# Six straight-line copies of the batch body become one hardware loop, on each of five engines

## The reference

```
x = x + 0.5 * ffn(layernorm(x))       # w_gate, w_up: 2048 x 512, w_down: 512 x 2048
x = x + attn(layernorm(x))            # 16 heads of 32, causal, unit-norm q and k,
x = x + 0.5 * ffn(layernorm(x))       # rotary embedding on the even heads, a gain per head

ffn(x)  = (silu(x @ w_gate.T) * (x @ w_up.T)) @ w_down.T
attn(x) = softmax(causal(q @ k.T * gain)) @ v @ w_out
```

## Time and profile before

| | |
|---|---|
| median of 3 runs | 3007.3 us (3006.99 to 3007.64) |
| the profiled execution | 3007.3 us, of which 3005.5 us lie between its first and its last instruction (the span) |
| instructions recorded | 56592 |
| PE | 2820.8 us busy, 94%, 23744 matmuls |
| PEld | 2056.7 us busy, 68% |
| DVE | 1806.0 us busy, 60%, 4252 instructions |
| ACT | 1222.2 us busy, 41%, 2218 instructions |
| POOL | 407.0 us busy, 14%, 438 instructions |
| DMA | 37.31 MB moved, of them 3.06 MB and 0.55 MB on the two queues of the kind "instruction" |

### The profile page before, as it was taken

How to read it: one execution, slowest core, us unless ns; L and a number is a source line. 1 busy time by engine, 2 the same in 40 slices (tenths; PEclk the granted TensorE clock), 3 DMA queues, 4 the chain that set the end, 5 groups by cost and what they waited for, 6 DMA issues and landing times.

```text
span 3005.5 us, 56592 instructions
## 1 busy us (share of the span) xinstructions
PE 2820.8 (94%) x23744; PEld 2056.7 (68%) x23744; DVE 1806.0 (60%) x4252; ACT 1222.2 (41%) x2218; POOL 407.0 (14%) x438
## 2 busy tenths in 40 slices
PE   4799999999999999999999999999999999999999
PEld 3576766676767667676776667776677676776666
DVE  8656766775357753667447674476634766357743
ACT  5233553552236522454225542254423553235522
POOL 0103203110022000220002200112002020021000
PEclk8899999999999999999999999999999999999999
DMA  6000000000000000000000000000000000000000
GB/s 240 15 1 1 2 1 1 8 1 22 1 1 9 7 17 1 1 8 22 1 1 1 8 22 1 1 1 8 22 1 1 8 1 22 1 1 9 1 8 15
DMA packets 15486, 37.31 MB, mean 12 GB/s; under 512 B 1408, under 2 KB 1408, under 8 KB 14720
## 3 DMA queue, kind: packets, MB, share of 16 engines
q1 hardware_dynamic: 15232, 33.70, 3.2%
HBM read 25.31 MB, written 8.39 MB: 11 GB/s over the span
## 4 chain that ended last, share of the span: by engine, by line
PE 66%; DVE 16%; ACT 9%; issue 6%; POOL 3%; DMA 0%; ACTq 0%; SPq 0%; DVEq 0%
PE psum L860 20%; PE psum L861 19%; PE psum L862 19%; ACT arena L567 5%; DVE mneg L771 3%; DVE arena L792 3%; ACT arena L563 2%; PE psum L905 1%; DVE arena L727 1%; PE psum L1016 1%; PE psum L968 1%; DVE arena L716 1%; PE psum L972 1%; DVE arena L723 1%; POOL rn L450 1%
## 5 line engine op out<-in xcount | busy, mean ns | idle before, releaser
L860 PE MATMUL psum<-arena,WG 128*128 128x256 f16 x2048 | 561.0, 274 | 14.7 <-DVE arena L716 14.7
L862 PE MATMUL psum<-arena,WG 128*128 128x256 f16 x2048 | 561.8, 274 | 0.0
L861 PE MATMUL psum<-arena,WG 128*128 128x256 f16 x2048 | 561.5, 274 | 0.0
L860 PE MATMUL psum<-arena,WU 128*128 128x256 f16 x2048 | 560.8, 274 | 0.0
L861 PE MATMUL psum<-arena,WU 128*128 128x256 f16 x2048 | 560.3, 274 | 0.0
L862 PE MATMUL psum<-arena,WU 128*128 128x256 f16 x2048 | 560.2, 274 | 0.0
L721 DVE SCALAR_TENSOR_TENSOR arena<-arena,psum 128x256 f32<-128x256 f32 x512 | 214.1, 418 | 493.2 <-ACT arena L578 492.6
L578 ACT ACTIVATE arena<-psum,tscale 128x256 f32<-128x256 f32 x512 | 242.4, 473 | 621.2 <-PE psum L862 620.7
L860 PE MATMUL psum<-WD,arena 128*128 128x512 f16 x1024 | 389.5, 380 | 38.9 <-DVE arena L727 38.9
L862 PE MATMUL psum<-WD,arena 128*128 128x512 f16 x1024 | 388.6, 379 | 0.0
L861 PE MATMUL psum<-WD,arena 128*128 128x512 f16 x1024 | 388.6, 379 | 0.0
(11 more groups left out here) (143 smaller groups left out, 4674.0 us busy)
## 6 DMA issues: line engine op xcount, KB each, us to landing
arena<-in_L_attn_x SPq DMA_DIRECT2D x16, 512.0 KB, 3.8
out<-arena SPq DMA_DIRECT2D x16, 512.0 KB, 2.8
arena<-in_L_ffn_w_gate SPq DMA_DIRECT2D x4, 1024.0 KB, 9.0
arena<-in_L_ffn_w_up SPq DMA_DIRECT2D x4, 1024.0 KB, 8.3
WD<-in_L_ffn_w_down SPq DMA_DIRECT2D x4, 1024.0 KB, 10.6
arena<-in_L_attn_w_qkv SPq DMA_DIRECT2D x1, 3072.0 KB, 20.8
WQ<-in_L_attn_w_out SPq DMA_DIRECT2D x1, 1024.0 KB, 23.1
ropet<-rope_table SPq DMA_DIRECT2D x1, 128.0 KB, 2.2
```

The costliest lines, as they stand in the source:

```text
L860: T_.matmul(o, lhs(0), rhs(0), start=first, stop=False)
L861: T_.matmul(o, lhs(0), rhs(1), start=False, stop=False)
L862: return T_.matmul(o, lhs(1), rhs(0), start=False, stop=last)
```

## The change

The six copies are replaced by one loop of six passes on each of the five engines. The body is written once, with `it` now a register and `ahead` fixed at 2, so that every value waited for in the body is computed from the register of the loop at run time. SP's loop over its four DMAs becomes a hardware loop too, with the DRAM addresses of `x[it + 2]` and `out[it + 1]` computed from the register.

```diff
--- before.py
+++ after.py
@@ -399,7 +399,7 @@
-            for it in range(B - 2):
+            with sp.Fori(0, B - 2) as it:
                 for th in range(2):
                     sp.wait_ge(s["x2_done"], it * TT + TT + 2 * th + 2)
                     sp.dma_start(xb[:, 2 * th:2 * th + 2, :], half_of(x[it + 2], th)).then_inc(s[f"x_in{th}"], 16)
@@ -491,8 +491,8 @@
             batch(0, 0, "first")
             batch(0, 1, "second")
-            for b in range(2, B):
-                batch(0, b, "loop")
+            with pool.Fori(0, B - 2) as it:
+                batch(it, 2, "loop")
@@ -597,8 +597,8 @@
-            for b in range(2, B):
-                batch(0, b, "loop")
+            with act.Fori(0, B - 2) as it:
+                batch(it, 2, "loop")
             batch(0, B, "last")
@@ -847,8 +847,8 @@
-            for b in range(2, B):
-                batch(0, b, "loop")
+            with dve.Fori(0, B - 2) as it:
+                batch(it, 2, "loop")
             batch(0, B, "last")
@@ -1062,8 +1062,8 @@
-            for b in range(2, B):
-                batch(0, b, "loop")
+            with pe.Fori(0, B - 2) as it:
+                batch(it, 2, "loop")
             batch(0, B, "last")
```

## The result

The changed kernel takes 3030.2 us, the median of 4 runs (3029.5 to 3033.9), against 3007.5 us for the kernel before, timed again beside it (each experiment below has its own such time, 3007.5 to 3008.1 us). The ratio is 1.0078, with a 95% interval of 1.006 to 1.0095: slower by 22.7 us. I had forecast 3010.5 us and a range up to 3028.

A forecast was written before the change was run, and what follows sets the result against it. PE's matmul stream was taken to bound each walk, except at some twenty waits on ACT/DVE chains. 3007.3 + 1.5 (jumps) + 2.7 (register instructions) - 1.0 (clock) = 3010.5 us, "no difference"; 8-in-10 range 3003 to 3028 us.

The forecast's parts named there:

- the jump is on the path: Rival, at a walk's end: DVE's sequencer not eight instructions ahead, or fetch over 2.2 us; 3018 us, chance 0.20.
- the restarts: Rival, at PE's waits: those held by register instructions cost up to 0.14 us each; 3027 us, chance 0.15.
- jumps, 5: Five jumps back on each engine between walks: 0.3 us each, 1.5 us in all, between 0 and 19.
- register instructions, 6 walks: Register instructions at PE's waits: 0.02 us for each of 23 waits a walk, 2.7 us in six.
- clock: At walks' ends: later PE start leaves less work at 1.2 GHz, winning back 1.0 of 4.2 us of delay.
- the cover in part one: At the jump: sequencers far enough ahead of DVE and PE to hide nearly all of a 2.2 us code fetch.
- the fetch: Loading code at a jump's target, taken as 2.2 us, the landing time of the smallest DMA shown.
- my less favourable reading: On PE, jump reached only when the transposes start (1060.29): code there at 1062.5, gate product 0.1 to 0.3 us late.
- the reading that DVE goes on 2.2 us late: At the jump, DVE's statistics not handed over early: DVE resumes at 1066.4, 2.2 us late, and PE's transposes with it.
- the low stretch: After each walk's end: 3.5 us with PE at 1.2 GHz, which a late start would leave partly idle.
- the worth of the stretch: At each walk's end: 1.6 us lost, as PE works at half speed during 3.20 us busy.

The follow-up runs named there:

- e1: The changed kernel with its register instructions and computed waits kept, but six walks laid out one after the other without jumps (SP as before): 3009.5 us, ratio 1.0006.
- e7: The changed kernel with spare matmuls in PE's idle time at a walk's end, 8 ahead of the second tile's transposes and 14 behind: 3023.6 us, ratio 1.0053.
- e6: The kernel before with spare matmuls in PE's idle time at a walk's end, 8 ahead of the second tile's transposes and 5 behind: 3003.2 us, ratio 0.9984.
- e4: The changed kernel with the loop on ACT, POOL and SP only; PE and DVE keep six straight copies: 3007.5 us, ratio 0.9998.
- e8: The changed kernel with DVE's and PE's loops cut in the feed-forward steps, four jumps in place of five: 3015.7 us, ratio 1.0027 to the kernel before.

## Why the prediction was wrong

The place was right, and so was its shape: a step "issue" on DVE and PE behind each walk's end, five times and not at the sixth. That was the rival *the jump is on the path*, to which I gave 0.20 and 3018 us. The rival nearest by its number, the restarts with 3027 us, is not what happened: e1 has every such wait and is 1.4 us above before. The terms, as predicted and measured:

| term | taken | measured | by |
|---|---|---|---|
| jumps, 5 | 5 x 0.3 = 1.5 us | 5 x 3.4 = 17 us | e7 less e6, less registers |
| register instructions, 6 walks | 2.7 us | 1.0 us | walks of e1 |
| clock | -1.0 us | about +5 us | 4.5 a walk in the changed kernel, less 3.4 and 0.2, five times |
| sum | 3.2 us | 23 us, of 22.7 | |

The step that failed is the cover in part one: "If DVE has them handed over at 1062.2 or earlier, the fetch ends by 1064.4". DVE had not. I took the 0.04 us between dependent instructions as a sign that the sequencer is ahead, and then let it be ahead by the eight instructions that I needed. The trace of the changed kernel has DVE's branch 0.09 us behind the start of the instruction before it, so it was ahead by one. On PE the place of the jump was as in my less favourable reading, 0.12 us behind the start of the transposes, but its branch took 4.0 us and the gate product came after 3.8 us without work in place of 1.5: 2.3 us late, not 0.1 to 0.3. The rows that I had could not tell one from eight, and the reading that DVE goes on 2.2 us late stood in the same paragraph; with DVE on the chain at the very jump, that end deserved the sum.

The second failure is the fetch: 2.98 us from branch to next instruction, not 2.2. I took the landing time of a small DMA as its value, and every stop over a long body, on every engine, was longer than that (2.4 us at the least, on ACT in e4).

The third is the sign of the clock's term. I argued that a late start moves slow work out of the low stretch. The stop makes PE's idle time longer instead, and the low stretch went from 3.5 us to 10.2. And the worth of the stretch, 1.6 us, was PE's half-speed work, without asking whether PE is what bounds it; e6 shows 0.5.

Two readings were wrong and changed nothing: the clock is under nine tenths in the first two slices, not four, and the first of the six walks takes 361.7 us, not 361.8.

What was right: computing unchanged; ACT's, POOL's and SP's jumps hidden (e4); register instructions among matmuls free, and at PE's waits nearly so (e1); PE's gate product covered in part by its wait.

## What to carry to other kernels

A hardware loop over a long body costs a stop of its sequencer at each jump back: here 2.8 to 3.6 us on DVE (789 instructions in the body, with the bare semaphore instructions), 2.4 to 4.3 on ACT (573) and 3.3 to 4.0 on PE (over 3000; up to 5.0 with the spare matmuls of e7 queued), while bodies of 74 instructions (POOL) and 12 (SP) cost 0.3 and 0.2 us, and the registers and the computed waits nearly nothing. No run tells at which length between 74 and 573 the stop begins. So don't ask whether to loop but where each engine's jump lies: put the cut of each engine's loop where that engine is idle anyway, which can be another place for each, and leave the bounding engine's copies straight. At the end of this pipeline's walk ACT and POOL had cover, and DVE and PE, through which the chain of dependent work runs, had not.

## What the runs showed that I had not expected

- The place in the stream from which DVE's and ACT's register instructions and branches are done is right behind the start of the instruction before them. PE's branch came 2.3 us ahead of the last matmul's start in e8, where PE had work queued.
- Spare matmuls of 2.8 us in PE's idle time kept the granted clock at 1.00 at all eight ends of a walk, and gave 4.3 us (0.14%) in a kernel that had not been changed otherwise.
- The five idle times of TensorE of 3.3 us in the mean, at the jumps, were followed by 6.8 to 13.7 us at 1.2 GHz; in the one shown TensorE was busy for 7.55 of the 10.2 us.
